# The end of a routed feed-forward layer: two gate-up units moved ahead of the downs, and the last expert's scaled rows ahead of a scaling

## What is computed

```python
h = tokens(x)
h = h + attention(layernorm(h))
n = layernorm(h)
combine = softmax weights of the two best of 7 experts, 0 elsewhere
mixed = sum over e of combine[:, e] * (silu(n @ wg[e]) * (n @ wu[e])) @ wd[e]
h = h + mixed + (silu(n @ sg) * (n @ su)) @ sd          # the shared expert
n = layernorm(h)                                        # the third norm
delta, value = sigmoid(n @ Wd.T + bd), n @ Wv.T + bv
h = h + scan(state = (1 - delta) * state + delta * value)
h = h + gated_square_relu(layernorm(h))                 # the last block
```

## Time and profile before

| what | us |
|---|---|
| median of 3 runs | 316.23 (316.22 to 316.68) |
| the profiled execution's own time | 318.52 |
| its span, first to last instruction | 316.5 |
| mean granted TensorE clock over the span | 0.999 |
| busy: PE, PEld | 304.6 (96%), 278.9 (88%) |
| busy: DVE, ACT, POOL | 192.7 (61%), 187.4 (59%), 157.9 (50%) |

### The profile page before, as it was taken

One profiled execution on the slowest core, in us unless ns is written; L12 is line 12 of the kernel. 1 busy time (PEld: TensorE's weight loads), 2 busy tenths in 40 slices (PEclk: granted clock), 3 DMA queues, 4 the chain that ended last, 5 costly groups with the idle time before them and its releaser, 6 DMA issues.

```text
span 316.5 us, 7394 instructions
## 1 busy us (share of the span) xinstructions
PE 304.6 (96%) x3094; PEld 278.9 (88%) x3094; DVE 192.7 (61%) x368; ACT 187.4 (59%) x324; POOL 157.9 (50%) x141
## 2 busy tenths in 40 slices
PE   8899999999999999999999999999999998999995
PEld 7776878889998999998999999999999998886673
DVE  1679135555654696747846776574838595736862
ACT  3485435756546685447597675847567463378761
POOL 6036013674442324464948686768585886200333
PEclk9999999999999999999999999999999999999999
DMA  7956226933000621549484848484757642000002
GB/s 246 412 138 188 77 75 198 276 134 119 2 4 2 199 68 68 183 144 292 133 288 117 285 116 278 145 267 162 265 167 223 198 157 85 22 4 0 1 0 81
DMA packets 32438, 46.03 MB, mean 145 GB/s; under 512 B 4272, under 2 KB 19728, under 8 KB 32400
## 3 DMA queue, kind: packets, MB, share of 16 engines
q1 hardware_dynamic: 30000, 41.71, 41.8%
q0 software_dynamic: 960, 2.43, 2.3%
q10 hardware_dynamic: 1440, 1.38, 1.4%
HBM read 38.22 MB, written 5.71 MB: 139 GB/s over the span
## 4 chain that ended last, share of the span: by engine, by line
PE 74%; DVE 8%; POOL 5%; ACT 4%; issue 3%; DMA 3%; SPq 1%; another core or an unknown queue 0%; DVEq 0%; POOLq 0%; ACTq 0%
PE ps L1578 19%; PE ps L1580 18%; PE ps L1579 18%; PE ps L1931 6%; PE ps L1731 3%; PE ps L1760 3%; PE ps L1600 3%; DMA v_region<-in_blocks 2%; PE ps L1593 2%; POOL v_region L569 2%; POOL w_lo L513 2%; DVE c_region L1021 2%; PE ps L1716 1%; DMA v_region<-expert_out,row_i 1%; DVE w_lo L1021 1%
## 5 line engine op out<-in xcount | busy, mean ns | idle before, releaser
L1578 PE MATMUL ps<-c_region,w_hi 128*128 128x224 f32 (+2 forms) x304 | 88.1, 290 | 1.2 <-DVE c_region L1021 1.1
L1579 PE MATMUL ps<-c_region,w_hi 128*128 128x224 f32 (+2 forms) x304 | 85.2, 280 | 0.0
L1580 PE MATMUL ps<-c_region,w_lo 128*128 128x224 f32 (+2 forms) x304 | 85.2, 280 | 0.0
L506 POOL TENSOR_TENSOR w_lo<-w_stage,w_hi 128x512 fp32r<-128x512 f32 x30 | 48.5, 1637 | 31.1 <-ACT w_hi L750 31.0
L1578 PEld LDWEIGHTS ps<-c_region,w_hi 128*128 128x128 f32 x304 | 58.1, 191 | 3.1 <-DVE c_region L1021 2.1
L1579 PEld LDWEIGHTS ps<-c_region,w_hi 128*128 128x128 f32 x304 | 58.1, 191 | 0.2
L1580 PEld LDWEIGHTS ps<-c_region,w_lo 128*128 128x128 f32 x304 | 58.0, 191 | 0.0
L750 ACT ACTIVATE w_hi<-w_stage 128x1024 fp32r<-128x1024 f32 (+1 forms) x42 | 49.7, 1196 | 2.6 <-DVE v_region L1423 2.6
L1021 DVE TENSOR_TENSOR c_region<-s_region,c_region 128x448 fp32r<-128x448 f32 (+1 forms) x44 | 37.4, 850 | 17.4 <-ACT c_region L877 11.6
L513 POOL TENSOR_TENSOR w_lo<-w_stage,w_hi 128x512 fp32r<-128x512 f32 x28 | 38.0, 1389 | 8.3 <-ACT w_hi L750 8.3
L1578 PE MATMUL ps<-xn_hi,w_hi 128*128 128x296 f32 x128 | 40.2, 314 | 0.9 <-DVE xn_lo L1021 0.7
(11 more groups left out here) (192 smaller groups left out, 604.4 us busy)
## 6 DMA issues: line engine op xcount, KB each, us to landing
w_stage<-in_w_gate SPq DMA_DIRECT2D x17, 512.0 KB, 4.9
w_stage<-in_w_up SPq DMA_DIRECT2D x17, 512.0 KB, 4.7
w_stage<-in_w_down SPq DMA_DIRECT2D x8, 1024.0 KB
expert_rows<-zeros SPq DMA_DIRECT2D x1, 1792.0 KB, 9.4
v_region<-in_blocks SPq DMA_DIRECT2D x6, 272.0 KB, 4.8
v_region<-expert_rows SPq DMA_DIRECT2D x1, 1344.0 KB, 8.2
expert_out<-v_region ACTq DMA_DIRECT2D x6, 224.0 KB, 4.7
w_stage<-in_w_v SPq DMA_DIRECT2D x1, 1024.0 KB, 7.3
```

The costliest lines, as they stand in the source:

```text
L506: w = g.tensor_tensor(wl[:, r], ws[:, r], wh[:, r].bitcast(F32), ALU.subtract)
L1578: mm(o, a_h, b_h, start=start, stop=False)
L1579: mm(o, a_h, b_l, start=False, stop=False)
L1580: return mm(o, a_l, b_h, start=False, stop=stop)
```

## The change

Only the order of instructions changes, on three engines.

- ACT: of the three scalings of second rows ahead of L905, the third moves behind L905's pair. Behind the last expert, both of the first two high parts come ahead of the fourth scaling, the fourth silu comes ahead of the third high part, and the square of the third norm comes ahead of the fourth high part, where it was behind.
- DVE: the first product moves ahead of the subtraction for the down weights. The fourth weighing moves behind the additions of merge(0); the centring moves ahead of the fourth product and of the third low part.
- PE: merge(0), back_down(0), gate-up 2, back_down(1), gate-up 3, mean, back_down(2), merge(1) with the variance inside, back_down(3) becomes merge(0), gate-up 2, gate-up 3, mean, back_down(0), back_down(1), merge(1) with the variance and back_down(2) inside, back_down(3).

```diff
@@ ACT
                     if final:
-                        for t in range(3):
+                        for t in range(2):
                             scale_second(t)
...
                             a.activation(yw_h[0:SP, st * D:(st + 1) * D], bank(4 + st, D)[0:SP, :], ACT.Copy,
                                          scale=slot_w[0:SP, st:st + 1]).then_inc(s["yw_hi"], 1)
+                        scale_second(2)
                         piece_high("dn", NX, KH // 2)
                         return
...
                 back_high(0)
+                back_high(1)
                 scale_second(3)
-                back_high(1)
                 back_silu(2)
                 scale_second(4)
+                back_silu(3)
                 back_high(2)
-                back_silu(3)
+                square(2, 0)
                 back_high(3)
...
-            square(2, 0)
             log_exp_tables()
@@ DVE
                         weigh(2)
+                        back_mul(0)
                         dve.wait_ge(hi_e["dn"], NX + 1)
...
-                back_mul(0)
                 back_mul(1)
                 back_low(0)
                 back_low(1)
-                weigh(3)
                 dve.wait_ge(s["merged"], 1)
                 add_merged(0, 0)
                 add_merged(1, 0)
+                weigh(3)
                 back_mul(2)
                 weigh(4)
+                centre(2, 0)
+                back_mul(3)
                 back_low(2)
-                back_mul(3)
-                centre(2, 0)
                 back_low(3)
                 normal(2, 0)
@@ PE
+                def variance_and_down():
+                    variance(2, 0)
+                    back_down(2)
...
                 merge(0)
-                back_down(0)
                 back_gate_up(2)
-                back_down(1)
                 back_gate_up(3)
                 mean(2, 0)
-                back_down(2)
-                merge(1, lambda: variance(2, 0))
+                back_down(0)
+                back_down(1)
+                merge(1, variance_and_down)
                 back_down(3)
                 last_layer()
```

## The result

The changed kernel takes **314.54 us** (median of 4, 314.02 to 314.7) where the kernel before takes 316.25 on the same chip. The ratio is 0.9933, 95% interval 0.9918 to 0.9949: 2.1 us faster, 1.6 to 2.6.

What follows compares the result with a forecast made beforehand. The prediction took the matmul engine, busy 96% of the span, as the bound. Gains of 0.55, 0.31 and 0.26 summed to 1.12 us, so 316.23 would become 315.1 us, with an 8-in-10 range of 313.4 to 316.3.

Steps and rivals of the forecast that it cites:

- four waits: Idle stretches of PE from the second back gate-up to the last layer's first product, together 2.72 us.
- (a): PE's wait between the second back gate-up and merge(0), 1.60 us; claimed to stay, gain 0, with g_y late.
- The first rival: g_y not late when timed: gain 2.72 us if only in the new kernel, 2.14 if in both; chance 0.20.
- 2.14: Gain in us claimed if g_y is on time in both kernels, giving 314.1 us.
- 0.58: ScalarE's idle us between third scaling and L905; the most (a) would shrink in the kernel before without the late signal.
- (b): PE's wait between merge(0) and back_down(0); claimed to go by putting gate-ups ahead of the downs, 0.55 us.
- (c): PE's wait ahead of the variance inside the second merge; claimed to go with two downs in between, 0.31 us.
- (d): PE's wait between the last down and the last layer's first product; claimed to go, 0.26 us.
- The covers: Slack before PE waits again, slimmest 0.22 us (table load before variance's result) and 0.55 (last layer); chance of failing 0.22.
- Slower: Rival: the fifth tile's last gather lands late and holds the norm, 317.0 us or more; chance 0.08.
- 2.29 us: Median 316.23 below the profiled execution's own 318.52; carried over unchanged into the forecast.

Runs made afterwards that it cites:

- after_gather_later: The changed kernel with the fourth tile's two gathers also issued behind yw_hi: 314.51 us, ratio 0.9939 to the kernel before.
- before_again: The kernel before, run once more without any edit for a second profile: 316.58 us against 316.53, ratio 1.0004.

## Why the prediction was right, and where not

**The bound and the waits.** Right: PE with four waits, all gone in the profile after.

**(a), the scaling.** The failed step is "(a) stays, gain 0", with its reason that everything before the signal is untouched. That everything before it is the same does not make the lateness the program's. In the executions that were timed the signal came on time; L905 then waited for the scaling, and moving it gave 0.73 to 0.85 us. The first rival had this, with 2.14 for the signal on time in both; the profiles gave 18.61 less 16.63, 1.98, and the two comparisons 2.1. The 2.14 is 0.16 too much because its 0.58 was too little: L905 starts 0.41 behind the scaling's start (264.53 to 264.94), not behind its whole 0.51, and the rows landed 0.07 earlier, so without the late signal L905 comes 0.75 sooner (+2.62 to +1.87).

**(b), (c), (d).** Right in kind and size. With the signal late the sum was 1.13 in the profile and 1.08 in the medians, for a forecast of 1.12. With it on time the same three were 1.98 less 0.85: 1.13. Within it (c) was worth 0.27 and not 0.31, for the variance's block takes 1.04 in the kernel after too, and (b) 0.58 with 0.14 taken off in place of 0.17.

**The covers.** The table load is over 0.20 before the variance (0.22 reckoned), and the wait is 0.26 when back_down(2) is taken out of its place (0.27). The drain that the Trainium skill (ScalarE: Activation LUTs, What ACT_TABLE_LOAD costs) adds to a switch did not show: the load ends at 275.91 and the logarithm waits for PE until 276.15, where 1.38 us more would have held it to 277.3.

**Slower.** Did not happen; the fifth tile's rows were there in time, and in after_gather_later even a wait of 1.41 us for them cost 0.05.

**The median against the profiled time.** I carried over the 2.29 us as it was. It was the clue: the profile read was of an execution with late signals, and the timed ones, by the numbers of before_again, had them on time. before_again's last down ends 1.60 earlier and its first block comes 0.76 sooner after it, 2.36 together, near the 2.29.

## What to carry to other kernels

When one profiled execution's own time is well above the median of the runs, look for waits that end well after the instruction that they are put down to, or that no engine of the core ends, and work the sum out both ways; here the median belonged to the case without them. An instruction's place behind a transfer's landing hides behind a later signal and shows its price when that signal comes on time. Orders written by hand on several engines form one schedule: PE's old order under the others' new one cost 3.6 us, more than the whole change gave.

## What the runs showed of the hardware

On one chip, in all four profiles taken there, and in the profile read for the prediction, PE's signal g_y reached ScalarE 2.3 to 2.6 us after the end of its matmul, while PE's own rows go on without a gap; in the seven profiles of other executions in which the last down gave the signal, L905 came 0.04 or 0.05 us behind it or straight behind the scaling. The last down ended at 264.2 to 264.8 in the first kind and at 262.9 to 263.3 in the second (the one that lost time in its first 100 us apart), so time is lost earlier too. The windows of 100 to 150 us show it, before and then after: 357 matmuls against 368 in the same time.

```profile
100.00:150.00 50.00, 49.08 (x357) 47.52 (x357) 34.71 (x85) 31.73 (x53) 21.49 (x19) 1.00 0.49 150
```

```profile
100.00:150.00 50.00, 50.00 (x368) 48.73 (x369) 35.41 (x86) 32.46 (x54) 22.87 (x20) 1.00 0.48 152
```

The kernel before took 318.23 on that chip and 316.2 to 316.6 elsewhere. The traces show where that time goes: a second signal from PE to ScalarE is late in the same five profiles and in no other. It releases a silu of the shared expert (L772). In the profile before, PE's matmul ends at 134.62 and the silu starts at 137.09, 2.47 us later (2.39 to 2.47 in the five); in the profile after, the matmul ends at 134.56 and the silu starts at 134.59:

```profile
137.09 0.42 ACT L772 ACTIVATE s_region<-ps 128x296 f32<-128x296 f32 x1 [2.49 <-PE ps L1580]
```

```profile
134.59 0.42 ACT L772 ACTIVATE s_region<-ps 128x296 f32<-128x296 f32 x1
```

At both signals GpSimd was issuing indirect transfers each time. That alone is not the cause, for it was issuing them at g_y in six of the seven profiles with the signal on time too; whether it has a part in it was only argued, and the run that was to test it fell on a chip with the signal on time. The cause stays open.
